# A recurrent network kernel: another order of the work in an LSTM cell, the state's sum one cell later, and a small cell of 256 and 128 columns

## The reference

```python
def step(carry, xt):
    h, c = carry
    g = xt @ Wx + h @ Wh + b
    i, f, gg, o = jnp.split(g, 4, axis=-1)
    c = sigmoid(f) * c + sigmoid(i) * jnp.tanh(gg)
    h = sigmoid(o) * jnp.tanh(c)
    return ((h, c), None)
...
m_from = lstm_last(base_emb[from_seq], seq_Wx, seq_Wh, seq_b)      # 64 steps
m_to = lstm_last(base_emb[to_seq], seq_Wx, seq_Wh, seq_b)
nwf = vmap(enc)(nwf_num_emb[fm], nwf_freq_emb[fm], ...)            # 11 features, 32 steps
...
return relu(feats @ reduce_W + reduce_b)
```

## Time and profile before

| | |
|---|---|
| median of 3 runs | 1969.59 us (1957.56 to 1969.84) |
| the profiled execution | 1965.39 us |
| its span, first to last instruction | 1963.6 us |
| mean granted TensorE clock | 0.966 of full speed |
| busy share of the span | PE 88%, DVE 72%, ACT 76%, POOL 47% |
| DMA, mean over the span | 279 GB/s |

### The profile page before, as it was taken

The page is one execution under the profiler, slowest core; times in us unless marked ns, Lnnn a source line. Parts: engine busy times, 40 slices in busy tenths (PEclk is TensorE's granted clock), DMA queues, the critical chain, the costliest instruction groups (busy, mean ns, idle before and its releaser), DMA issues.

```text
span 1963.6 us, 60788 instructions
## 1 busy us (share of the span) xinstructions
PE 1728.5 (88%) x25604; PEld 806.0 (41%) x25604; DVE 1410.2 (72%) x1279; ACT 1499.2 (76%) x2707; POOL 930.3 (47%) x476
## 2 busy tenths in 40 slices
PE   2169899999999899998998999999999999999994
PEld 1123344444444444443444444444444444444443
DVE  7067677677777777777777777787777777877771
ACT  2246778788888788887888788888888887888783
POOL 7348854444444444444454344444544444444442
PEclk9579999999999999999999999999999999999997
DMA  6699999989899999999899899998998998899941
GB/s 171 110 315 301 289 295 289 286 297 313 296 286 293 298 295 301 293 302 288 290 300 305 282 295 307 303 310 287 299 302 283 302 307 304 292 291 306 288 163 44
DMA packets 170255, 548.66 MB, mean 279 GB/s; under 512 B 53214, under 2 KB 58624, under 8 KB 124928
## 3 DMA queue, kind: packets, MB, share of 16 engines
q1 hardware_dynamic: 167423, 544.63, 89.5%
q0 software_dynamic: 2560, 0.15, 0.7%
HBM read 536.95 MB, written 7.54 MB: 277 GB/s over the span
## 4 chain that ended last, share of the span: by engine, by line
PE 61%; ACT 18%; issue 6%; DVE 1%; DMA 1%; SPq 0%; POOL 0%; ACTq 0%; POOLq 0%
PE ab L607 29%; PE e_ps L541 16%; PE f_ps L607 8%; ACT gate L658 7%; PE ab L568 6%; ACT tanh_c L658 5%; PE ab L506 2%; ACT gate L666 1%; ACT seq_x L512 1%; ACT gate L668 1%; ACT f_ps L666 1%; ACT f_ps L668 1%; DVE hot L531 1%; DMA last_h<-nwf_h 0%; PE e_ps L893 0%
## 5 line engine op out<-in xcount | busy, mean ns | idle before, releaser
L694 POOL TENSOR_TENSOR ig<-gate 128x1024 f32<-128x1024 f32 x192 | 411.1, 2141 | 948.8 <-ACT gate L666 617.2
L553 DVE SCALAR_TENSOR_TENSOR kept<-high,cst,e_ps 128x1024 f32<-128x1024 bf16 x352 | 449.5, 1277 | 285.1 <-issue 264.3
L541 PE MATMUL e_ps<-hot,tab 128*32 128x512 bf16 x8448 | 531.6, 386 | 31.3 <-issue 17.9
L531 DVE TENSOR_SCALAR hot<-low,cst 128x4096 bf16<-128x4096 bf16 x352 | 440.8, 1289 | 3.6 <-DMA low<-low_digits 3.6
L607 PE MATMUL ab<-seq_h,seq_wh 64*64 64x512 f32 x3072 | 405.7, 595 | 0.0
L666 ACT ACTIVATE gate<-ab 128x1024 f32<-128x1024 f32 x256 | 262.0, 1024 | 144.5 <-PE ab L607 141.5
L541 PEld LDWEIGHTS e_ps<-hot,tab 128*32 128x32 bf16 x8448 | 195.7, 97 | 379.6 <-issue 156.0
L727 POOL TENSOR_TENSOR seq_h<-gate,tanh_c 128x1024 f32<-128x1024 f32 x128 | 303.0, 2367 | 0.0
L658 ACT ACTIVATE gate<-ab 64x512 f32<-64x512 f32 (+1 forms) x384 | 227.8, 593 | 35.6 <-PE ab L607 32.6
L658 ACT ACTIVATE tanh_c<-seq_c 64x512 f32<-64x512 f32 (+1 forms) x384 | 241.7, 630 | 3.8 <-DVE seq_c L712 0.8
L668 ACT ACTIVATE gate<-ab,nwf_bias 128x256 f32<-128x256 f32 (+3 forms) x448 | 156.8, 428 | 82.2 <-PE ab L607 80.6
(11 more groups left out here) (76 smaller groups left out, 1724.5 us busy)
## 6 DMA issues: line engine op xcount, KB each, us to landing
low<-low_digits SPq DMA_DIRECT2D x352, 1024.0 KB
high<-high_digits SPq DMA_DIRECT2D x1408, 64.0 KB
tok<-seq_tokens SPq DMA_DIRECT2D x128, 512.0 KB, 7.6
nwf_in<-in_r_nwf_numbers SPq DMA_DIRECT2D x1, 2816.0 KB, 13.5
nwf_in<-in_r_nwf_freqs SPq DMA_DIRECT2D x1, 2816.0 KB, 20.7
low_digits<-turned SPq DMA_DIRECT2D x8, 352.0 KB, 6.0
high_digits<-turned SPq DMA_DIRECT2D x8, 320.0 KB
low<-last_h SPq DMA_DIRECT2D x11, 64.0 KB
```

The costliest lines, as they stand in the source:

```text
L531: nc.vector.tensor_scalar(hot[:, p % HOT_RING, :, :].rearrange("p u c -> p (u c)"), low[:, p % LOW_RING, :, :].rearrange("p u c -> p (u c) ...
L541: last = nc.tensor.matmul(e_ps[32 * g:32 * g + 32, i, :], tab[:, part, 2 * m + ty, :], hot[:, p % HOT_RING, i, g * CH:(g + 1) * CH], start ...
L553: nc.vector.scalar_tensor_tensor(out=kept[:, p % KEPT_RING, :, :].rearrange("p u c -> p (u c)"), in0=high[:, p % HIGH_RING, :, :].rearrang ...
L694: nc.gpsimd.tensor_tensor(ig[:, n % 2, 0:w], gates[0][:, n % 2, 0:w], gates[1][:, n % 2, 0:w], ALU.mult).then_inc(ig_ready, 1)
```

## The change

The order in a cell is new on PE, ACT and DVE. PE: first lookup, X, **SX**, gates g and i, **last lookup**, gate f, gate o. ACT copies SX right after X, ahead of gate g, and `USES` has it there. DVE: **`add_c` of the cell before**, then for each pair K and C of the pair **two** on, then `seq_compare` of the step **one further on** than before, then `scale_c`. At the start three `seq_compare` and two C run ahead of the cells, and SP loads the tokens of one more step ahead of them. POOL's wait is for the `seq_compare` that its cell now has, one step further on. Part 1 (N1) has a block of 256 columns (features 9 and 10) and one of 128 (feature 8) in place of two of 192 that cut a feature pair in two, so each gate has 8 matmuls in the code and not 12, and each of its activations fewer pieces. The buffers are flat in place of [block, column]; in PSUM the two blocks stand next to each other around column 512.

```diff
+PARTS = [((0, 512, ((0, 0, 256), (1, 256, 256))), (512, 512, ((2, 0, 256), (3, 256, 256)))),
+         ((1152, 256, ((5, 0, 256),)), (1024, 128, ((4, 0, 128),)))]
-SEGMENTS = [([(0, 0, 256), (1, 256, 256)], [(2, 0, 256), (3, 256, 256)]),
-            ([(4, 0, 128), (5, 128, 64)], [(5, 0, 192)])]
...
+COMPARED = AHEAD + 1
...
     USES += [("x", _r, _m) for _r, _m in SETS_AT[_n]]
-    USES += [("gate", _n, 0), ("gate", _n, 1), ("gate", _n, 3)]
     if later_seq(_n) is not None:
         USES.append(("sx", later_seq(_n)))
+    USES += [("gate", _n, 0), ("gate", _n, 1), ("gate", _n, 3)]
...
 def _(sp):
-                for s in range(2, 4):
+                for s in range(2, 2 + COMPARED):
                     load_tokens(sp, s)
...
-                    if s is not None and s + 2 < 2 * SEQ_T:
-                        load_tokens(sp, s + 2)
+                    if s is not None and s + 1 + 2 < 2 * SEQ_T:
+                        load_tokens(sp, s + 1 + 2)
...
 def _(dve):
-                compare_pair(dve, 0)
+                for p in range(HOT_RING):
+                    compare_pair(dve, p)
+                for s in range(AHEAD, COMPARED):
+                    seq_compare(dve, s)
                 for n in range(NCELLS):
                     if n < 4:
                         place_nwf_w(dve, *divmod(n, 2))
-                    pairs = PAIRS_AT[n]
-                    for p in pairs[:-1]:
+                    if n:
+                        add_c(dve, n - 1)
+                    for p in PAIRS_AT[n]:
                         keep_wanted(dve, p)
-                        compare_pair(dve, p + 1)
-                    if len(pairs) == 1:
-                        keep_wanted(dve, pairs[0])
-                    if pairs and pairs[-1] + 1 < ALL_PAIRS:
-                        compare_pair(dve, pairs[-1] + 1)
-                    if later_seq(n) is not None:
-                        seq_compare(dve, later_seq(n))
-                    if len(pairs) > 1:
-                        keep_wanted(dve, pairs[-1])
+                        if p + HOT_RING < ALL_PAIRS:
+                            compare_pair(dve, p + HOT_RING)
+                    if later_seq(n) is not None and later_seq(n) + 1 < 2 * SEQ_T:
+                        seq_compare(dve, later_seq(n) + 1)
                     scale_c(dve, n)
-                    add_c(dve, n)
+                add_c(dve, LAST)
...
 def _(pool):
-                    if later_seq(n) is not None:
-                        pool.wait_ge(seq_hot_ready, later_seq(n) + 1)
+                    if later_seq(n) is not None and later_seq(n) + 1 < 2 * SEQ_T:
+                        pool.wait_ge(seq_hot_ready, later_seq(n) + 2)
                     input_product(pool, n)
...
 def _(act):
                     for r, m in SETS_AT[n]:
                         store_x(act, r, m)
+                    if later_seq(n) is not None:
+                        seq_store_x(act, later_seq(n))
                     activate(act, n, 0)
...
                     activate(act, n, 3)
-                    if later_seq(n) is not None:
-                        seq_store_x(act, later_seq(n))
...
 def _(pe):
                     for r, m in SETS_AT[n]:
                         set_input(pe, r, m)
+                    if later_seq(n) is not None:
+                        seq_lookup(pe, later_seq(n))
                     gate(pe, n, 0)
                     for p in pairs[1:-1]:
                         look_up(pe, p)
                     gate(pe, n, 1)
-                    gate(pe, n, FORGET)
                     if len(pairs) > 1:
                         look_up(pe, pairs[-1])
+                    gate(pe, n, FORGET)
                     gate(pe, n, 3)
-                    if later_seq(n) is not None:
-                        seq_lookup(pe, later_seq(n))
```

More of the change, by code:

```diff
@@ L1 @@
 from contextlib import ExitStack
+from itertools import zip_longest
 import numpy as np
@@ L583, in gate @@
             place = GATES[g][0]
-            h = h_blocks(n)
+            h = h_of(n)
+            wp = widths(n)[0]
             if g == 0:
@@ L597, in gate, with tiles @@
                 bank = begin_use(pe, ("gate", n, g))
-            def tiles(lhs, rhs_p, rhs_q, cols_p, cols_q, start, stop):
-                for block, rhs, cols, swap in ((0, rhs_p, cols_p, 0), (1, rhs_q, cols_q, 1)):
-                    if rhs is None:
+            def tiles(lhs, rhs, spans, start, stop):
+                for block, span in enumerate(spans):
+                    if span is None:
                         continue
+                    a, b = span
                     for half in range(2):
@@ L605, in tiles @@
                         rows = slice(64 * half, 64 * half + 64)
-                        to = 64 * (half ^ swap)
-                        last = nc.tensor.matmul(bank[to:to + 64, block, cols], lhs(half, block), rhs(rows),
-                                                start=start, stop=stop)
-                return last
+                        to = 64 * (half ^ block)
+                        cols = slice(CH - wp + a, CH - wp + b) if block == 0 else slice(CH + a, CH + b)
+                        last = nc.tensor.matmul(flat(bank)[to:to + 64, cols], lhs(rows, half, block),
+                                                rhs(rows, block, a, b), start=start, stop=stop)
@@ L611, in gate, with h_rhs @@
+                return last
+            def h_rhs(rows, block, a, b):
+                return h[rows, wp * block + a:wp * block + b]
             if kind == "seq":
                 x = seq_x[:, (2 * step + k) % X_RING, :, :]
[L613 to L617, removed]
+                every = ((0, CH), (0, CH))
+                tiles(lambda rows, half, block: seq_wx[rows, place, :],
+                      lambda rows, block, a, b: x[rows, block, a:b], every, True, False)
+                last = tiles(lambda rows, half, block: seq_wh[rows, place, :], h_rhs, every, False, True)
@@ L618, in gate @@
             else:
-                at, w = NWF_AT[k]
                 x = nwf_x[:, step % 2, :]
[L621 to L640, removed]
@@ new lines, in gate @@
+                for sets in zip_longest(*(block[2] for block in PARTS[k])):
+                    spans = [s and (s[1], s[1] + s[2]) for s in sets]
+                    tiles(lambda rows, half, block: nwf_w[rows, 1 - half, sets[block][0], place, :],
+                          lambda rows, block, a, b: x[rows, PARTS[k][block][0] + a:PARTS[k][block][0] + b],
+                          spans, True, False)
+                    last = tiles(lambda rows, half, block: nwf_w[rows, half, sets[block][0], place, :],
+                                 h_rhs, spans, False, True)
@@ L645, in pieces, with at_h @@
             kind, _, k = CELLS[n]
+            wp = widths(n)[0]
             if kind == "seq":
[L647 to L653, removed]
+                return [(block, CH * block, CH, None) for block in range(2)]
+            return [(block, wp * block + a, c, nwf_bias[:, m, GATES[g][0]:GATES[g][0] + 1])
+                    for block in range(2) for m, a, c in PARTS[k][block][2]]
+        def at_h(to, of, parts, function):
+            for block, a, c, bias in parts:
                 for half in range(2):
@@ L657, in at_h @@
                     if block or not half:
-                        last = nc.scalar.activation(to(rows, slice(w * block + cols.start, w * block + cols.stop)),
-                                                    of(there, block)[:, cols], function,
+                        last = nc.scalar.activation(to[rows, a:a + c], of[there, a:a + c], function,
                                                     bias=0.0 if bias is None else bias[there, :])
@@ L666, in in_place @@
                 return nc.scalar.activation(to, of, GATES[g][1])
-            for block, cols, bias in pieces(n, g):
-                last = nc.scalar.activation(to[:, block, cols], of[:, block, cols], GATES[g][1], bias=bias)
+            for _, a, c, bias in pieces(n, g):
+                last = nc.scalar.activation(to[:, a:a + c], of[:, a:a + c], GATES[g][1], bias=bias)
             return last
         def activate(act, n, g):
-            w = width(n)
             what = ("gate", n, g)
```

71 lines of the change are left out of this document (34 added, 37 removed).

## The result

The changed kernel takes 2005.67 us (median of 4 runs, 2005.22 to 2020.33) against 1963.57 for the kernel before (the 3 runs of the table above and one more): 1.0243 times, with a 95% interval of 1.0164 to 1.0323. It is slower by 2.4%. The profiled execution took 2005.77 us with a span of 2004.0, 40.4 us more than the span before.

The account below looks back on a forecast made before the run. PE bounds the kernel (88% busy), with about 2 us of ACT waits a round. 27 rounds by 1.6 (43), first rounds +4, stops −4, start +10, last N cells −1: +52, plus 4 for the median, 2020 us; range 1945 to 2050.

Parts of the forecast that it names:

- the start: Ahead of the first K: it waits behind the third `seq_compare` and its tokens, +10 us (bounds 0 and 13).
- the stops: Single stops of PE across the run: partly taken up by the new waits, −4 us.
- The ring: Sequence cells: last lookup, K, C, `seq_compare`, POOL's product, `add_c`, next K; 9.83 us, 0.60 longer than PE's cell.
- A round: One round of the loop: 56.4 us, 1.6 longer than 54.84, with a wait at N1's gate f.
- PE's own cell: PE's work in a sequence cell: 9.08 us plus a 0.15 wait for SX, 9.23 in all.
- the wait of gate i for SX: PE in four S cells: gate i waits for ACT's copy of SX, 0.15 us each, 0.6 a round.
- PE alone: A round set only by PE and its waits on ACT would need 54.1 us.
- The new blocks: N1's gates on PE: 0.86 us each, +0.64 a round; ACT saves some 0.8 a cell off the path.
- The port: Rival, N0: POOL's product holds off DVE's C at the shared port, +0.85 us a round; 2046 us, chance 0.12.
- The ring has room: Rival: `seq_compare` or POOL come some 0.6 us sooner, PE sets the pace at 54.1 a round; 1957 us, chance 0.18.
- the best: Rival: waits on ACT go, SX costs nothing, the start is caught up; 53.1 us a round, 1915 us, chance 0.10.
- Loads: SP's loads: still some 14 us ahead of use; 16.6 MB in a 56.4 us round ask for less than before.

Follow-up runs that it names:

- The early compare: The changed kernel with `seq_compare` moved ahead of the last keep on DVE, POOL's wait kept: 1964.34 us, ratio 1.0028 to the kernel before.
- an SP edit: The changed kernel with SP loading the third step's tokens right behind the first pair, not behind four: 1996.01 us, ratio 1.0169 to the kernel before.
- the versions that cut the ring: The changed kernel with `seq_compare` ahead of the last keep, 1964.34 us; the same with the third step's tokens and the first cells' `new_h` also earlier, 1968.85 us.

## Why the prediction was right

The forecast was 2020 and 2000 to 2040 around it, the median is 2005.67. The direction and the mechanism held; two terms of the sum were mis-sized with opposite signs, the start by +20 and the stops by −35. That the median lies inside 2000 to 2040 is luck in part: with the stops as forecast it would have been 2041, with the start as forecast 1986.

- **The ring.** Forecast 9.83 us from last lookup to last lookup, measured 9.84; POOL released by the compare in 123 cases; moving the compare alone took a quiet round from 56.5 to 54.28, with the product mostly released by ACT again. The early compare is the shown half of the argument; that POOL's wait closes the ring is right too, but it doesn't follow that a round gets shorter without it: there it is 64 us or more.
- **A round.** Forecast 56.4, measured 56.50. Inside it PE's own cell was sized too long: the waits of S1 and S1' are 0.95 and not 0.60. A lookup ahead of X takes 1.31 where I had 1.55, and the wait of gate i for SX is about 0.1 and not 0.15. The ring fixes the round, so this had no effect. Gate f of N1 waits 0.83, forecast 1.1; SX of S0' waits 0.70 for ACT, forecast 0.3. PE alone was put at 54.1; the early compare's quiet rounds are 54.28. The right sum hides two wrong halves: the order alone makes a quiet round 57.0, where I expected 56.1 in that run, and the new blocks take off 0.5 where I had them as a cost.
- **The new blocks** were the step that I didn't understand. I priced them as +0.64 of PE a round and ACT's saving as off the path. Measured they take 0.5 off a quiet round in either order (54.84 to 54.36, 57.0 to 56.5). Alone they make the kernel 1.2% faster, above all because they end the stops.
- **Single stops, −4.** Measured −39.3, this and the few late loads together. I had them down as partly hidden by new waits and didn't ask where they stood; all but one stood in or behind N1, which the timeline before the change shows, and all end 1.3 to 1.7 us after an instruction packet lands. The two parts of the change each shorten them: of PE's idle time without a releaser 9.8 us are left with the blocks alone, and with the order alone 13.2, leaving out the wait for a new h.
- **The start, +10.** Measured +30.0. The late first K was right (126.5, forecast behind 123.7; POOL's first product at 137.4, forecast 134), and an SP edit brings 11.6 back. The other half I left out: in the first step there are no N cells, so a sequence cell needs the h of two cells before, not three. That `new_h` stands behind POOL's product and so behind the compare: a second ring of 14.1 us a cell (192.03 to 206.15 above), with four waits of 3.6 to 3.9 us. Putting `new_h` first took 13.3 us back (15.0 less the 1.7 of an earlier start). Moving the compare ahead of the last K opens this ring as well, and brings 20 back by itself.
- **The rivals.** The port: C began first and POOL was the one held up (3.10 against 2.37), and the round came out at the ring's sum, so at no cost that shows, as forecast for that order. I took its price from the pair of compares in the earlier trace rows, 0.17 for 0.36 of overlap, as small. In the run without POOL's wait it is whole instructions. The Trainium skill, "SBUF — State Buffer", section "SBUF: two separate sides", states just this: whichever of the two starts first holds the shared pair for the whole instruction. The run without the wait agrees with it (C ended 1.09 us after the product, where it takes 1.28 alone); in N0 the product was held up 0.73 for an overlap of 0.88, a little less than the rule gives. "The ring has room" and "the best" fell with the first round measured.
- **Loads.** I wrote that a round of 56.4 asks for less than before and left it there. That holds at 56.5 (5.3 us of waits). It decides what can be won: near 54.3 the same bytes come late sooner or later, and the versions that cut the ring end no lower than before the change.

## What to carry to other kernels

Before moving an operation, close the ring through every engine that waits for it: the compare was cheap in both places, but behind the last keep it made a cycle of DVE, POOL and PE that is 0.6 to 0.95 us longer than PE's cell. Follow the ring through the start as well, where the distance between steps is shorter than later. And look at where the disturbances stand, not only at how long they last in total: a part of the change that looked like a small cost ended the stops, and alone was the one worth keeping.

## What the runs showed of the hardware

- A DVE compare in bf16 and a POOL product that meet take turns: 1.28 became 2.85 us, 0.75 became 2.83, and 2.37 became 3.34 on POOL. The kernel in which they were left free to meet in every sequence cell is 11% slower than the changed one and 14% slower than before, the lower granted clock (0.95 to 0.97 in its rounds) included.
- PE stops of 1.5 to 3.9 us without a semaphore stood behind runs of 24 matmuls of 64 to 192 columns in 0.7 us. They are late instructions: in all 14 a 16 KB packet of the instruction queue lands 1.25 to 1.66 us before PE goes on. With 16 matmuls in 0.86 us only two of 1.0 and 1.7 us were left, and with the old blocks and a fifth of the load traffic left out they fell to 1.6 us or less.
- The loads are a bound of their own close below 55 us a round. Rounds of 54.3 us move 302 to 315 GB/s, and with all loads each version that ran at this pace had low digits coming late in the end; in such a stretch the DMA engines were busy throughout at 287 GB/s and a load took 18.8 us to land.
